# Two AdaLN blocks over 16 samples: the first sample's score maxima taken from fp32 products, angle and rotor tables made later, up parts of its experts bounded on VectorE

## The reference

```
# layer 0, attention: 16 heads of 8, with a relative term
scores = (content + rel) / sqrt(8)          # 256 x 256 for each head
attn   = softmax(scores)                    # out = attn @ v, then Wout
# layer 0, feed-forward: 16 experts, the best 4 of each token
gate = minimum(gu[..., ::2], 7)
up   = clip(gu[..., 1::2], -7, 7)
act  = (up + 1) * gate * sigmoid(1.702 * gate)
out  = sum_e score_e * (act_e @ down_e + bias_e)
# layer 1, attention: running sums over time with rotors exp(i t f), then Wo
# layer 1, feed-forward: sigmoid(r) * (relu(k)^2 @ W_v)
```

## Time and profile before

| | us |
|---|---|
| median of 3 runs (lowest to highest) | 1451.95 (1451.33 to 1452.53) |
| the profiled execution | 1452.62 |
| its span in the trace | 1450.9 |
| head, to the end of the last score maximum | 54.05 |
| first, to the end of the last expert product | 131.4 |
| one step, most of them | 82.5 to 82.9 |
| PE, DVE, ACT, POOL busy | 84%, 78%, 68%, 19% |

### The profile page before, as it was taken

One profiled execution on the slowest core, in us unless ns is written; L12 is line 12 of the kernel. 1 busy time (PEld: TensorE's weight loads), 2 busy tenths in 40 slices (PEclk: granted clock), 3 DMA queues, 4 the chain that ended last, 5 costly groups with the idle time before them and its releaser, 6 DMA issues.

```text
span 1450.9 us, 22142 instructions
## 1 busy us (share of the span) xinstructions
PE 1215.8 (84%) x6834; PEld 903.2 (62%) x6834; DVE 1129.5 (78%) x2122; ACT 992.0 (68%) x1716; POOL 276.6 (19%) x260
## 2 busy tenths in 40 slices
PE   3667898888889898888989888898988888798887
PEld 2345575756757575665757566675756667575665
DVE  6435979798897969889796988979697897969765
ACT  1446786867677786767778676777767677776741
POOL 2312130311213120221312022131302113130210
PEclk9979999999999989999998999999899999989998
DMA  5321020303011030301103030210303021020000
GB/s 116 94 25 12 10 26 9 33 8 32 8 17 19 5 33 8 33 8 19 21 5 29 8 33 8 21 19 6 27 8 33 8 23 17 8 25 5 1 5 4
DMA packets 54663, 29.94 MB, mean 21 GB/s; under 512 B 3741, under 2 KB 53610, under 8 KB 54634
## 3 DMA queue, kind: packets, MB, share of 16 engines
q1 hardware_dynamic: 52744, 28.87, 16.1%
q10 hardware_dynamic: 1890, 0.70, 0.5%
HBM read 8.20 MB, written 2.10 MB: 7 GB/s over the span
## 4 chain that ended last, share of the span: by engine, by line
PE 42%; ACT 23%; issue 15%; DVE 14%; DMA 2%; POOL 1%; ACTq 1%; SPq 0%; DVEq 0%; POOLq 0%
PE ring L712 11%; PE pa L726 7%; DVE smax L1722 6%; PE pa L646 4%; PE ring L633 4%; ACT prob L1266 3%; ACT L1299 2%; PE ring L699 2%; PE pb L812 2%; ACT prob L1202 2%; ACT gsc L1255 2%; DVE prod L1827 2%; PE pb_k L742 2%; ACT frac L1302 2%; ACT sin_t L1299 2%
## 5 line engine op out<-in xcount | busy, mean ns | idle before, releaser
L712 PE MATMUL ring<-ht,wgu 128*128 128x256 f32 x1024 | 256.4, 398 | 10.6 <-ACT prob L1266 9.8
L417 POOL TENSOR_TENSOR gsc<-gsc,sc_all 128x512 f32<-128x512 f32 x128 | 167.8, 1316 | 405.2 <-ACT gsc L1260 405.2
L712 PEld LDWEIGHTS ring<-ht,wgu 128*128 128x128 f32 x1024 | 199.9, 199 | 53.9 <-ACT gsc L1255 13.5
L1854 DVE TENSOR_TENSOR_SCAN prod<-keep,prod 128x512 f32<-128x512 f32 x188 | 223.6, 1210 | 0.0
L1787 DVE SCALAR_TENSOR_TENSOR prob<-prob,gsc 128x512 f32<-128x512 f32 x128 | 86.7, 686 | 139.8 <-POOL gsc L417 89.4
L1722 DVE TENSOR_REDUCE smax<-ring 128x4 f32<-128x1024 f32 x128 | 153.0, 1218 | 19.5 <-PE ring L610 16.7
L812 PE MATMUL pb<-prod,wo 128*128 128x256 f32 x544 | 129.3, 382 | 18.9 <-DVE prod L1868 18.9
L1202 ACT ACTIVATE prob<-ring 128x1024 f32<-128x1024 f32 x128 | 125.7, 1023 | 8.7 <-PE ring L633 7.1
L1255 ACT ACTIVATE gsc<-ring,gub_t 128x256 f32<-128x256 f32 x256 | 110.1, 499 | 24.7 <-PE ring L712 24.7
L726 PE MATMUL pa<-prob,wdown 128*128 128x256 f32 x512 | 122.5, 381 | 4.7 <-DVE prob L1787 4.7
L812 PEld LDWEIGHTS pb<-prod,wo 128*128 128x128 f32 x544 | 102.0, 190 | 35.0 <-DVE prod L1868 21.8
(11 more groups left out here) (269 smaller groups left out, 2367.3 us busy)
## 6 DMA issues: line engine op xcount, KB each, us to landing
q_rows<-qk_part SPq DMA_DIRECT2D x144, 64.0 KB
k_rows<-qk_part SPq DMA_DIRECT2D x135, 64.0 KB
x_in<-in_L_attn_x_dram SPq DMA_DIRECT2D x16, 128.0 KB, 2.2
sc_all<-_L_ffn_gate_up_proj_dram SPq DMA_DIRECT2D x1, 2048.0 KB, 12.2
out_dram<-xo SPq DMA_DIRECT2D x16, 128.0 KB, 1.8
prob<-in_L_wmod_dram SPq DMA_DIRECT2D x2, 384.0 KB, 4.1
k_rows<-qk_part ACTq DMA_DIRECT2D x9, 64.0 KB
wo<-in_L_attn_Wo_dram SPq DMA_DIRECT2D x1, 512.0 KB, 7.4
```

The costliest lines, as they stand in the source:

```text
L417: pool.tensor_tensor(gsc[:, n % NG, :], gsc[:, n % NG, :], sca, ALU.mult).then_inc(S["gsc"], 1)
L712: last = mm(ring[:, n % 2, g * 512 + j * L:g * 512 + (j + 1) * L], lhsT=wgu[:, 2 * n + j, g, :], rhs=ht[:, :], start=True, stop=True, skip ...
L1854: nc.vector.tensor_tensor_scan(prod[:, h, n - 1, :], keep[:, :], prod[:, h, n - 1, :], 0.0, ALU.mult, ALU.add).then_inc(S["cu" + str(n)], 1)
```

## The change

**Maxima of sample 0.** In `head` the score groups no longer use the copied rows. DVE makes one column per head that is 1 in the head's eight partitions and 0 elsewhere (`head_of`), and `heads_first` multiplies q by each of the columns: heads 0 to 11 on DVE, 12 to 15 on ACT. `scores_first` multiplies these 128-row copies (`q_head`, in the memory of `wgu`) with k in fp32, 4 products a group, 8 groups, while the row copies are under way. All 8 maxima, where there were 5, stand in `head`. The split into parts keeps `qk` intact (`rest_first`, `part_first`). POOL's copies into `wgu` wait for the last of these groups. PE waits for the copied rows (`rows_landed`) only ahead of `scores_t`.

**Later work.** The modulations' products (PE), their 12 small operations, `small_tables` and `angles` (DVE) follow the maxima; `turn_weights` becomes three pieces with waits of their own. The sines, absolute values and cosines are made on ACT in `first`: the sines after `copy_values`, the others around `second_norm_2`. The rotor turns stand ahead of `turn_scores` (three) and among the experts (five), DVE's copies with them. `memory_weights` stands behind the last `up_first`, ahead of the last two pair products on DVE. `down_scaled` stands behind `copy_broadcast`.

**Experts of sample 0.** `up_first` (DVE, two instructions from PSUM) adds a bias and takes the minimum; `last_first` takes the maximum and multiplies in one instruction. ACT's `up` and `clip_up` are gone from `first`.

**Loads.** W_r, W_k, W_v are loaded ahead of the 2 MB gate/up weights; SP's wait for all row copies stands behind `spread_max`.

SP, POOL and PE:

```diff
+        head_of = rden[:, 0, :]
+        q_head = wgu[:, :, :, :].rearrange("p e g d -> p (e g d)").rearrange("p (h l) -> p h l", l=L)
+        qk_rest = frac[:, :, :].rearrange("p a n -> p (a n)")[:, 0:2 * L].rearrange("p (n l) -> p n l", n=2)
...
+                for n, w in enumerate((W_r, W_k, W_v)):
+                    sp.dma_start(ffn_raw[:, n, :], w).then_inc(SET["ld_f"], 16)
                 sp.dma_start(sc_all[:, :, :], gup.rearrange("e h f -> h e f")).then_inc(SET["ld_gu"], 16)
                 spread_first()
+                spread_max(nx)
                 sp.wait_ge(S["qk_rows"], 16 * 18)
-                for n, w in enumerate((W_r, W_k, W_v)):
-                    sp.dma_start(ffn_raw[:, n, :], w).then_inc(SET["ld_f"], 16)
-                sp.dma_start(wout[:, :], Wout).then_inc(SET["ld_w"], 16)
-                sp.dma_start(wrout[:, :], router_w).then_inc(SET["ld_w"], 16)
+                sp.wait_ge(SET["ld_f"], 16 * 3)
+                sp.dma_start(wout[:, :], Wout).then_inc(SET["ld_f"], 16)
+                sp.dma_start(wrout[:, :], router_w).then_inc(SET["ld_f"], 16)
...
+            def rest_first(b):
+                need(pool, "part0", b, 1)
+                pool.tensor_tensor(qk_rest[:, :, :], qk[:, :, :], qk_part[:, 0, :, :], ALU.subtract).then_inc(S["rest0"], 1)
...
             def expert_weights():
-                pool.wait_ge(*upto("dve", "ang"))
...
                 pool.wait_ge(SET["ld_gu"], 16)
+                need(pool, "s_ps", 0, ST)
...
-                rest_q(nx)
-                rest_q_2(nx)
+                rest_first(nx)
+                rest_first_2(nx)
...
+            def turn_ffn():
                 pe.wait_ge(SET["ld_f"], 16 * 3)
+                pe.wait_ge(*upto("dve", "gub_t"))
                 for n in range(3):
                     last = tr(pb[:, n * D:(n + 1) * D], ffn_raw[:, n, :], ident[:, :])
-                last.then_inc(*mark("pe", "bd_ps"))
+                last.then_inc(*mark("pe", "ffn_ps"))
...
+            def rows_landed(b):
+                need(pe, "qk_rows", b, 16 * 18)
+
+            def mods_copied():
+                pe.wait_ge(*upto("dve", "mod_rest"))
...
             def weights_loaded():
-                pe.wait_ge(SET["ld_w"], 16 * 5)
+                pe.wait_ge(SET["ld_f"], 16 * 5)
...
+            def scores_first(b, n):
+                if n == 0:
+                    need(pe, "q_sb", b, 1)
+                    need(pe, "k_sb", b, 1)
+                if n < 3:
+                    pe.wait_ge(*upto("dve", "qm%d" % n))
+                if n == 3:
+                    pe.wait_ge(*upto("act", "qm3"))
+                if n >= 2:
+                    need(pe, "s_max", b, n - 1)
+                for j in range(4):
+                    last = mm(ring[:, n % 2, j * L:(j + 1) * L], lhsT=q_head[:, 4 * (n % 4) + j, (n // 4) * P:(n // 4 + 1) * P],
+                              rhs=qk[:, 1, :], start=True, stop=True, skip_group_check=True)
                 last.then_inc(S["s_ps"], 1)
...
-                modulations(0, 2, 6, "m1_ps")
-                modulations(1, 0, 6, "m2_ps")
-                pe.wait_ge(*upto("dve", "mod_rest"))
-                scores(nx, 0)
-                scores(nx, 1)
-                scores(nx, 2)
-                scores(nx, 3)
-                scores(nx, 4)
-                scores(nx, 5)
-                scores(nx, 6)
+                scores_first(nx, 0)
...
+                scores_first(nx, 7)
...
             def first(a, nx):
-                scores(a, 7)
                 turn_max(a)
-                turn_weights()
+                maxima_read(a)
+                modulations(0, 2, 6, "m1_ps")
+                modulations(1, 0, 6, "m2_ps")
+                turn_inv()
+                turn_bias()
+                turn_ffn()
                 values_free()
-                turn_rotors(0)
-                turn_rotors(1)
-                turn_rotors(2)
+                mods_copied()
+                rows_landed(a)
                 scores_t(a, 0)
                 scores_t(a, 1)
                 values(a, 0)
                 scores_t(a, 2)
                 values(a, 1)
```

ACT, cut (`heads_first` makes heads 12 to 15 by four copies with the column as scale; `rotor_abs` is the middle instruction of the three):

```diff
-                part_2(nx)
+                heads_first(nx)
+                part_first(nx)
                 spread_first()
-                rotor_sines()
-                rotor_cosines()
...
                 copy_values(a, 1)
-                down_scaled()
+                rotor_sines()
                 attn_tail(a)
                 attn_tail_2(a)
                 head_1(nx)
                 second_norm_1(a)
                 head_2(nx)
+                rotor_abs()
                 second_norm_2(a)
+                rotor_cosines()
                 part(nx)
                 part_2(nx)
                 route(a)
@@ -1472,38 +1536,23 @@
                 copy_broadcast(a, 1)
                 copy_broadcast(a, 2)
                 copy_broadcast(a, 3)
+                down_scaled()
                 gate_clip(a, 0)
...
                 bend(a, 0)
-                clip_up(a, 0)
-                up(a, 1)
                 gate_clip(a, 1)
-                clip_up(a, 1)
...
```

DVE:

```diff
+                dve.wait_ge(*upto("pool", "ident"))
+                nc.vector.tensor_reduce(head_of[:, :], ident[:, :].rearrange("p (d h) -> p h d", h=H), AX_X, ALU.add)
...
+            def heads_first(b):
+                need(dve, "q_sb", b, 1)
+                for n in range(3):
+                    for h in range(4 * n, 4 * n + 4):
+                        last = ts(q_head[:, h, :], qk[:, 0, :], head_of[:, h:h + 1], None, ALU.mult)
+                    last.then_inc(*mark("dve", "qm%d" % n))
...
+                dve.wait_ge(*upto("dve", "gub_t"))
+                ts(up_b[:, :], gub_t[:, 1, :], -1.0, LIMIT + 1.0, ALU.mult, ALU.add).then_inc(*mark("dve", "up_b"))
+                dve.wait_ge(*upto("pe", "ffn_ps"))
...
+            def up_first(b, n):
+                need(dve, "gu_ps", b, n + 1)
+                need(dve, "dn", b, n - NU + 1)
+                for j in range(2):
+                    ts(upc[:, n % NU, j * L:(j + 1) * L], ring[:, n % 2, 512 + j * L:512 + (j + 1) * L],
+                       up_b[:, 2 * n + j:2 * n + j + 1], LIMIT + 1.0, ALU.add, ALU.min).then_inc(S["uprl"], 1)
+
+            def last_first(b, n):
+                need(dve, "uprl", b, 2 * n + 2)
+                need(dve, "gsc", b, n + 1)
+                stt(out=upc[:, n % NU, :], in0=upc[:, n % NU, :], scalar=1.0 - LIMIT, in1=gsc[:, n % NG, :],
+                    op0=ALU.max, op1=ALU.mult).then_inc(S["act"], 1)
...
                 head_5(nx)
+                heads_first(nx)
                 head_6(nx)
-                constants_2()
-                modulations()
-                small_tables()
-                angles()
                 maxima(nx, 0)
                 maxima(nx, 1)
+                constants_2()
                 maxima(nx, 2)
...
+                maxima(nx, 7)
...
             def first(a, nx):
-                maxima(a, 5)
-                maxima(a, 6)
-                maxima(a, 7)
                 split_max(a)
+                modulations()
+                small_tables()
                 weights()
-                rotor_table(0)
-                rotor_table(1)
-                rotor_table(2)
                 next_a(a)
+                angles()
                 stats_and_mod(nx)
-                rotor_table(3)
-                rotor_table(4)
-                rotor_table(5)
-                rotor_table(6)
-                rotor_table(7)
                 normal(nx)
-                memory_weights()
                 attn_norm(a)
                 centre(a, "2", x1, cent, pa)
                 epsilon(a, "2", veps, pa)
                 scale(a, "2", cent, pa)
                 head_5(nx)
                 route(a)
+                rotor_table(0)
+                rotor_table(1)
+                route_2(a)
                 head_6(nx)
-                route_2(a)
-                expert_last(a, 0)
-                expert_last(a, 1)
-                expert_last(a, 2)
-                expert_last(a, 3)
-                expert_last(a, 4)
-                expert_last(a, 5)
-                expert_last(a, 6)
-                expert_last(a, 7)
+                rotor_table(2)
+                up_first(a, 0)
+                up_first(a, 1)
+                rotor_table(3)
...
+                up_first(a, 6)
+                last_first(a, 5)
+                up_first(a, 7)
+                memory_weights()
+                last_first(a, 6)
+                last_first(a, 7)
```

86 lines of the change are left out of this document (59 added, 27 removed).

## The result

| | before | after |
|---|---|---|
| median (lowest to highest), us | 1452.24 (1451.33 to 1453.91) | 1444.51 (1442.45 to 1446.42) |
| the profiled execution | 1452.62 | 1442.45 |
| its span in the trace | 1450.9 | 1440.7 |
| q of sample 0 written from | 15.59 | 14.70 |
| last score maximum ends | 54.01 | 34.87 |

Ratio of the medians 0.9945, 95% interval 0.9925 to 0.9965: 7.7 us faster. The profiled executions lie 10.2 us apart. The forecast was 12.5 to 12.6. The four runs of after stand in two pairs, 1442.45 and 1442.86, 1446.15 and 1446.42; the distance between the pairs is 3.6 on average. That is near what one step in which the clock falls costs (4.1), but only the first of the four runs was profiled, so no trace shows what sets the pairs apart.

The account below looks back on a forecast made before the run. The prediction took a chain of single waits in the first 131 us as the bound; -16.2 + 1.75 - 0.7 + 2.5 = -12.6 us, from the median 1451.95 to about 1439.5, range 1432 to 1447.

Parts of the forecast that it names:

- (c): Rival, chance 0.06: the fp32 score products stay at half pace, 12.7 us of the gain are gone, 1452 us.
- (d): Rival, chance 0.04: each half product costs 0.505 us as in head_5, a group 4.04, the whole about 1457 us.
- (e): Rival, chance 0.05: row copies, with the maxima's DMA and later weights behind them, land late; 1443 us at the outside.
- Step 1: Sample 0's score maxima under the row copies: last maximum at 35.7 us, split and transpose to 37.2, 11.1 us hidden.
- (b): Rival, chance 0.19: less lost to the clock, 1435.5 to 1437 us; small loads may land sooner, up to 2 us.
- Step 2: Behind the maxima: the weights' path decides, transposed scores start at 45.8 us not 61.6, -15.8 (bounds 44.3 and 48).
- step 6: Clock behind down_pair 5, where PE idles: about half of the next step's stretch runs slowly, +2.5 us (0 to 4.1).
- Step 3: Angles on DVE's path behind the transposed scores: attn_out_1 starts at 62.2 us instead of 78.4, -16.2.
- Step 4: Router of sample 0: cosines +0.45 and the exponent's table load +1.28, together +1.75 us.
- Step 5: Experts of sample 0, with memory_weights ahead of the last two pair products: down_pair 7 ends at 130.7, -0.7 us.
- The rule on POOL and DVE: Shared port in the head: POOL's split could wait for DVE's scalings, copies land at 45.6 us, time unchanged.
- (a): Rival, chance 0.18: in the steps the clock's falls begin one turn earlier, 5 falls instead of 4, +4.1, 1443.6 us.

Follow-up runs that it names:

- e6: Changed kernel with sample 0's maxima taken again from the copied rows by bf16 products, most of the head scalings gone: ratio 1.0075 to before.
- e17: Changed kernel with POOL's two operations of the split of q and k waiting for DVE's last scaling of q: ratio 0.9957 to before.
- e1: Changed kernel with POOL's copies of the gate/up weights behind the split of the maxima instead of beside it: ratio 0.9948 to before.
- e3: Changed kernel with ten unread fp32 products on PE between the last score group and turn_max: ratio 0.9955 to before.
- e13: Changed kernel with the 20 remaining modulation products on PE between q and k's products and the first score group: ratio 0.9920 to before.
- e8: Changed kernel with sample 0's attn_norm ahead of sample 1's normalisation on DVE: ratio 0.9946 to before.
- e9: Changed kernel with an unread one-column exponent on ACT between the two copies of sample 1's split, loading the table there: ratio 0.9951 to before.

## Why the prediction was right, and where not

The time came to 1444.5 for a forecast of 1439.5, inside its range. The mechanism was right: e6 shows that the maxima under the copies carry the gain, rivals (c) and (d) are refuted by the last four groups, 1.73 us apart, and (e) by the landing at 41.8. But two of the signs that the prediction had named for being wrong came true: the first transposed scores waited past 48 (49.05), and the slow steps weren't four. Sizes were off. Two stretches came out 3.4 and 3.3 us worse than forecast, two others 1.0 and 3.3 better, so that the sum missed by only 2.4. That these nearly cancelled is in part luck:

| us, shift against before | forecast | measured |
|---|---|---|
| attn_out_1 | -16.2 | -12.75 |
| from there to gate_up 0 | +1.75 | +0.7 |
| from there to sample 0 leaving | -0.7 | +2.6 |
| behind that | +2.5 | -0.8 |
| sum | -12.6 | -10.2 |

**Step 1** was right: from q to the last maximum 20.17 us, forecast 20.1. The mark itself came 0.8 sooner (34.87 for 35.7), as q came 0.9 sooner. Rival (b) had this in part: the rows that PE's products for q wait for landed by 7.8 and not at 12.1, and PE had its part at 11.2 and not at 15.5. But then DVE's other wait held q, for dbias, which landed at 14.62, about where it had in before (issued at 6.34, 8.2 us to landing), so only 0.9 of 4.3 was left. The scalings took 5.28 for a forecast of 3.3; e17 shows that this was not on the path.

**Step 2 failed by 3.25 us**, 4.1 when counted from the last maximum (14.18 for 10.1), in two of its terms. "Split and transpose take 1.5 us as before", on which it stands, took the rows of before without looking who would run beside them: the change itself puts POOL's copies there, because they wait for the last score group. That cost 2.4 (e1). And the 2.4 us for the modulations' products assumed the full clock; they ran at the half (4.45). The text had a bound for exactly that, a start at 48, but took the good end: the 4.94 us in which PE waits for the split were not weighed as an idle stretch, though the prediction did weigh one of 4.7 in step 6. e3 shows that the clock was the cause. Without the first error the second would have been smaller and not gone: in e1 the split takes its 1.2 us and the products 3.23. The choice of what is late next, the weights' path and not the DMA, was right (e13).

**Step 3** was right: from the transposed scores to attn_out_1 16.60 us, forecast 16.4, with DVE's angles deciding (e8: attn_norm sooner, attn_out_1 sooner).

**Step 4** had the price of the table load and the cosines right: +1.75 forecast, +1.58 measured from attn_out_1 to the exponent. It missed that the later exponent takes exm away from POOL's remainder (1.12 to 0.26, -0.86; e9 shows both halves). On the draining of 1.38 us that the Trainium skill (ScalarE: Activation LUTs, What ACT_TABLE_LOAD costs) adds to a switch: the load starts at 79.55, takes 1.28, and the exponent starts at 80.85. No draining is seen, and the row was the right price.

**Step 5 failed by 3.3 us.** gate_up 7 ended 23.1 us behind gate_up 0 for a forecast of 22.55. Then memory_weights took 4.75 until DVE was free again, not 3.9: one of the 16 scalings took 1.29 beside a POOL product. And the two last down_pairs took 3.78 at the half clock.

**Step 6** had the right event in the right place, but a wrong price list. The clock fell at 115.6, in PE's wait. The forecast laid its cost on the third norm and the first phases of the next step; it was paid at once, 1.9 us in the two down_pairs, and then the level rose at 122.4. The first step took 82.6 us, as before (82.5). So the 2.5 forecast in the last line of the table and 1.9 of what the line above it measured are one event, counted on the other side of a mark.

**The rule on POOL and DVE.** The prediction quoted the Trainium skill (SBUF — State Buffer, SBUF: two separate sides) on the scalings alone and gave it no time. The rule's form is borne out: a DVE operation waits until the POOL operation ends. Its place was wrong: it was DVE that lost and not the copies, and it counted at the split, where the prediction did not look.

**The steps.** Rivals (a) and (b) counted slow steps of 86.9. After has three of about 86.7 and two of 84.4, the first of them already the second step. So the clock falls in five steps and begins earlier, as (a) had it, but the sum is 14.8 us against 15.7 in before, so its +4.1 did not come. Of (b), the gap of step 6 did lower the clock, and no step fewer was touched. In the other runs this part moved by up to 5 us in both directions.

## What to carry to other kernels

When work is hidden under a transfer, price what follows it with the neighbours that it will have afterwards: an engine that is released by the same event is a new neighbour. A POOL operation between SBUF tiles beside short DVE operations costs DVE up to the POOL operation's length each time it starts (0.7 to 1.7 us here, for POOL operations of 1.3 to 2.0); move it behind them, or to ACT if that is idle. Where a gap of PE is on the path, count the products behind it at the half clock (4.45 us for 2.77 and 3.78 for 1.9 here). And read a gain of a few us at marks in the trace, not in medians, at several marks, and against runs whose clock changes at the same places: runs with the same code between two marks differed by 0.8 us here.
